# Attention's last batch: the exponents' sums made on TensorE instead of GpSimd

## The reference, cut to what matters

```python
q, k, v = proj(layernorm(x), W_Q, b_Q), proj(ctx, W_K, b_K), proj(ctx, W_V, b_V)
scores = einsum('bhqd,bhkd->bhqk', q, k) / sqrt(32)
attn = softmax(scores, axis=-1)         # over the 512 keys
out = einsum('bhqk,bhkd->bhqd', attn, v)
x = x + tanh(g_xattn[0]) * (out @ W_O + b_O)
# then a quantized FFN, a second attention on the raw context, and a quantized linear layer
```

## Time and profile before

| | us |
|---|---|
| median of 3 runs | 1707.97 (1707.79 to 1710.96) |
| the profiled execution, its own time | 1708.97 |
| its span, first to last instruction | 1707.2 |
| of it up to the end of the attention phase | 839.9 |
| PE busy | 1513.5 (89%) |
| DVE busy | 1233.4 (72%) |
| POOL busy | 905.9 (53%) |
| ACT busy | 873.6 (51%) |

### The profile page before, as it was taken

The page is one execution under the profiler, slowest core; times in us unless marked ns, Lnnn a source line. Parts: engine busy times, 40 slices in busy tenths (PEclk is TensorE's granted clock), DMA queues, the critical chain, the costliest instruction groups (busy, mean ns, idle before and its releaser), DMA issues. The chain is left out here.

```text
span 1707.2 us, 25251 instructions
## 1 busy us (share of the span) xinstructions
PE 1513.5 (89%) x7272; PEld 981.8 (58%) x7305; DVE 1233.4 (72%) x2149; ACT 873.6 (51%) x1433; POOL 905.9 (53%) x1162
## 2 busy tenths in 40 slices
PE   4799999998999999998446899999999939999997
PEld 3556666665656666663135455555555417888885
DVE  3567776777767776666374688888888717999985
ACT  3255555555555555554365545555555415555552
POOL 3168566676658566666301433443444115777774
PEclk9899999999999999997667999999999969999998
DMA  5827456473827456470271444444444353445420
GB/s 187 256 63 207 145 159 194 130 216 111 244 79 204 146 157 198 118 204 13 98 272 37 78 107 113 111 110 106 113 111 110 66 185 118 137 148 182 139 68 37
DMA packets 198430, 233.90 MB, mean 137 GB/s; under 512 B 97196, under 2 KB 114104, under 8 KB 194744
## 3 DMA queue, kind: packets, MB, share of 16 engines
q1 hardware_dynamic: 198328, 232.68, 47.3%
HBM read 135.86 MB, written 75.53 MB: 124 GB/s over the span
## 5 line engine op out<-in xcount | busy, mean ns | idle before, releaser
L510 ACT ACTIVATE a_probs<-a_sc 128x512 f32<-128x512 f32 x512 | 300.3, 596 | 298.7 <-PE a_sc L423 296.2
L565 DVE TENSOR_REDUCE a_negmax<-a_mx 128x1 f32<-128x512 f32 x512 | 338.0, 675 | 99.2 <-PE a_mx L406 98.3
L619 POOL TENSOR_TENSOR a_acc<-a_acc,a_probs 128x512 f32<-128x512 f32 x256 | 320.9, 1283 | 6.0 <-ACT a_probs L510 4.4
L619 POOL TENSOR_TENSOR a_acc<-a_probs 128x512 f32<-128x512 f32 x128 | 161.7, 1284 | 243.5 <-ACT a_probs L510 242.6
L406 PE MATMUL a_mx<-a_stack 96*128 96x512 f32 x512 | 227.0, 443 | 32.9 <-DVE a_negmax L565 20.8
L1002 PE MATMUL bank<-w_wgu,b_xq 128*128 128x512 bf16 x1022 | 227.7, 381 | 7.6 <-DMA b_xq<-b_xcode 7.6
L423 PE MATMUL a_sc<-a_stack 97*128 97x512 f32 x512 | 216.2, 424 | 9.5 <-DMA a_stack<-a_mrow 7.5
L571 DVE RECIPROCAL a_attn<-a_den 128x128 f32<-128x128 f32 x128 | 120.8, 948 | 121.5 <-PE a_den L444 121.5
L1002 PEld LDWEIGHTS bank<-w_wgu,b_xq 128*128 128x128 bf16 x1024 | 100.4, 98 | 130.0 <-DMA b_xq<-b_xcode 8.5
L406 PEld LDWEIGHTS a_mx<-a_stack 96*128 96x128 f32 x512 | 100.8, 197 | 102.1 <-DVE a_negmax L565 51.1
L1041 ACT ACTIVATE b_sig<-bank,b_tok 128x512 f32<-128x512 f32 x128 | 87.6, 684 | 92.4 <-PE bank L1002 89.2
(11 more groups left out here) (177 smaller groups left out, 2733.2 us busy)
## 6 DMA issues: line engine op xcount, KB each, us to landing
a_stack<-spill SPq DMA_DIRECT2D x192, 256.0 KB, 4.9
spill<-a_part SPq DMA_DIRECT2D x64, 512.0 KB, 3.4
ctx_t<-a_ct SPq DMA_DIRECT2D x16, 1024.0 KB, 8.5
c_ct<-ctx_t SPq DMA_DIRECT2D x8, 2048.0 KB, 8.1
a_stage<-in_x_dram SPq DMA_DIRECT2D x32, 256.0 KB, 5.0
a_stage<-in_ctx_dram SPq DMA_DIRECT2D x32, 256.0 KB, 2.7
attn_t<-a_attn SPq DMA_DIRECT2D x32, 256.0 KB, 3.0
b_xin<-in_x_dram SPq DMA_DIRECT2D x32, 256.0 KB, 2.7
```

The lines of the kernel that those rows point to most:

```text
L510: nc.scalar.activation(probs[:, k, j, :], sc[i % 2][:], ACT.Exp, scale=SCALE).then_inc(exp_done, 1)
L565: nc.vector.tensor_reduce(negmax[:, g % 2, j, t:t + 1], mx[i % 2][:], axis=AX.X, op=ALU.max, negate=True).then_inc(mx_done, 1)
L619: nc.gpsimd.tensor_tensor(acc[:, j], probs[:, 0, j] if k == 1 else acc[:, j], probs[:, k, j], ALU.add)\
```

## The change

In the last batch alone, PE makes the whole sum. A new function `add_up(k)` multiplies the block of ones by the exponents of key tile k, four matmuls into the four strips of `den`, accumulating over the key tiles.

```diff
+                def add_up(k):
+                    for j in range(J):
+                        last = nc.tensor.matmul(den[DH * j:DH * (j + 1), :], ones[:], probs[:, k, j, :], start=k == 0, stop=k == T - 1)
+                    return last
...
                     elif name == "pv":
...
+                        if it + shift == NB - 1 and k < T - 1:
+                            if k == 0:
+                                wait_count(pe, recip_done, it, shift, G * T, g * T)
+                                wait_count(pe, mt_done, it, shift, G, min(g + 2, G))
+                            add_up(k)
...
                     elif name == "den":
                         g, = args
+                        if it + shift == NB - 1:
+                            add_up(T - 1).then_inc(den_full, 1)
+                            return
...
                     elif name == "score":       # ACT
-                        wait_count(act, acc_done, it, shift, G * (T - 1) * J, ((g - 1) * (T - 1) + max(k, 1) - 1) * J + j + 1)
+                        if it + shift < NB - 1 or g == 0:
+                            wait_count(act, acc_done, it, shift, G * (T - 1) * J, ((g - 1) * (T - 1) + max(k, 1) - 1) * J + j + 1)
+                        elif k == T - 1 and j == 0:
+                            wait_count(act, den_full, it, shift, G, g)
...
-                    elif name == "acc":         # POOL
+                    elif name == "acc" and it + shift < NB - 1:
```

## The result

The changed kernel takes 1716.05 us (median of 6 runs, 1712.39 to 1720.94), the kernel before, with three more runs beside it, 1708.93 (6 runs, 1707.14 to 1714.24). The ratio of the runs is 1.004, with a 95% interval of 1.0024 to 1.0057: slower by 7 us, between 4 and 10. The prediction was 1716.1, with +8.1 us: the difference is 1 us smaller than forecast, and that the median meets 1716.1 almost to the digit is luck, since the kernel before had 1707.97 when the forecast was made and has 1708.93 with all six runs. The profiled execution has a span of 1714.2 us, 7.0 more than before.

The account below looks back on a forecast made before the run. The last batch was taken as a serial chain of TensorE bursts and scoring stretches. Added sets +10.4, removed GpSimd waits −2.6 and moved waits +0.3 gave +8.1 us, so 1716.1 us, with 8 in 10 for 1712 to 1720.

Parts of the forecast that it names:

- The chain is serial: Last batch: bursts and scoring stretches follow one another, so whatever lengthens a TensorE burst is paid in full.
- The price of a set: Last batch's bursts: four den matmuls of one key tile cost 0.865 us; twelve added sets cost 10.4 us.
- The upper bound of 12.9: Bursts: 0.105 us per change of bank would raise added sets to 12.9 us; dearer sets in general had chance 0.14.
- The removed waits: Before den in groups 1 and 3: waits of 0.75 and 1.83 us for GpSimd's adds go, −2.6 us.
- The moved wait for the copied maxima: Burst starts, groups 0 to 2: first den set waits for the copied maxima, 0.1 us each, +0.3 in all.
- The clock: Last batch: added sets fall on the bursts' upper-clock part, at 0.865 us; time at the lower level does not grow.
- The rise comes inside the burst in every case: Groups 1 to 3: the clock rises within the burst, which begins with 1.1, 4.5 and 3.9 us at the lower level.
- The stretches: Three scoring stretches between bursts: change taken as 0, upper end 1.5 us; lengths near 15.2, 14.5 and 11.0 us.
- The sum: Whole last batch: +8.1 us from added sets, removed waits and moved waits; chance 0.72 for +5.5 to +10.5.
- the clock stays up by denser bursts: Rival, last batch: denser bursts keep the upper clock through the stretches, −1.3 us, 1706.7; chance 0.11, wholly or in part.
- GpSimd was the real bound: Rival, bursts: GpSimd's adds set their length, so removing them pays for the sets; 1706 to 1709 us, chance 0.03.

Follow-up runs that it names:

- e4: Changed kernel with every set of den matmuls in the last batch made twice, sixteen sets more; 1728.58 us, 12.5 over the changed kernel.
- e2: Changed kernel with the last batch's sums left out, only one key tile multiplied by the ones; 1705.59 us, 3.1 under the kernel before.
- e3: Changed kernel with TensorE making the sums in all eight batches, GpSimd adding nothing; 1784.98 us, 76.3 over the kernel before.
- e5: Changed kernel plus one unused full-width matmul behind each score matmul of the last batch's groups 1 to 3; 1709.84 us, 6 under the changed kernel.
- e7: Changed kernel with pv sets of groups 0 to 2 moved behind the next stretch's first four scores, group 3's sets between its scores; 1713.93 us.
- e1: Changed kernel with GpSimd's 48 last-batch adds made as well, their result unused; 1717.16 us, 8.4 over the kernel before.
- e9: Kernel before, GpSimd's sums kept, plus one unused matmul behind each score matmul of the last batch's groups 1 to 3; 1712.63 us.
- e6: Kernel before, but last batch's group 3 summed by TensorE, with den and pv sets of key tiles 0 to 2 between its score matmuls; 1702.45 us.
- e8: Kernel before with group 3's sets between scores; in groups 1 and 2 GpSimd adds three key tiles, with unused matmuls behind scores; 1702.32 us.

## Why the prediction was right, step by step

**The chain is serial.** Right. Sixteen sets more gave +13.1 us of the way (e4), twelve fewer −10.2 (e2), and eighty-four more, those of the seven other batches, +68.9 by the medians (e3), which is 0.82, 0.85 and 0.82 us each.

**The price of a set, 0.865 at the upper clock.** Right: 2.57 us for three (7.00 of e5's burst against 4.43), 10.3 for twelve. The upper bound of 12.9, with a price on each change of bank, is refuted by the even 0.86 between starts above. The Trainium skill ("TensorEngine Tiling (Array Packing)", Key Properties) says that the engine is drained when the tiling mode changes, not when only the tile does. The runs agree on both sides: nothing is paid between `den` and `pv`, and in e7 a set alone between full-width matmuls takes 1.00 us (774.66 to 775.66) instead of 0.86. What the 0.14 us are made of no run separates.

**The removed waits, −2.6.** Right in kind, as e1 (nothing else in GpSimd's work) and e2 bear out, and some 0.3 us too small. The two idle times, 0.75 and 1.83, are counted from modelled ends. In the kernel before, the `pv` matmuls ahead of these waits are

```profile
785.33 4.14 PE L434 MATMUL a_pvb<-a_probs,a_v 128*32 128x512 f32 x32
...
823.41 5.58 PE L434 MATMUL a_pvb<-a_probs,a_v 128*32 128x512 f32 x32
```

and in group 0, where nothing waits, such a row is 3.64 us long and the next starts 3.46 after it, 0.18 before its modelled end. So `den` could have started 3.96 and 5.40 us after these two starts. It started 4.89 and 7.40 after them (790.22 and 830.81), 0.93 and 2.00 late: 2.9 us in all. And the waits are a figure of this clock: e9 has 10.1 us of idle time there.

**The moved wait for the copied maxima.** I took 0.3 us. From the score matmul ahead to the burst's first start it is 0.33 us before and 0.36 after in group 0, and 0.71 and 0.80 in group 2: some 0.1 in all. Group 1 can't be compared, since the clock there differs.

**The clock.** Half right. That longer bursts carry their sets at the upper level held: the time at the lower level in the bursts was 9.5 us before and is 10.1 (0.26 × 2 × 9.43 and 0.27 × 2 × 9.67). "The rise comes inside the burst in every case" was wrong. In group 1 the clock rose ahead of it:

```profile
788.00:789.00 1.00, 1.00 (x5) 0.62 (x4) 0.84 (x2) 0.60 (x1) 0.00 (x0) 0.65 0.00 0
```

That is most of why group 1's burst took 7.01 and not the 7.9 I gave it. Group 3 had more at the lower level (9.67 for 9.3), and group 2 came out as forecast (9.43 for 9.4).

**The stretches.** I left them as they were; they came out 0.71 us shorter together (14.68, 14.61, 10.71 for 15.18, 14.53, 11.00), which I had not forecast. e1 and e4 have them at 15.17, 14.63 and 11.00 with the same sets or more, so the sets are not the cause. The rows show where the time went. In the first stretch TensorE is without a gap from these starts on, the first in the kernel before, the second in the changed one:

```profile
779.78 0.71 PE L406 MATMUL a_mx<-a_stack 96*128 96x512 f32 x1
...
784.40 0.71 PE L412 MATMUL a_mx<-a_stack 96*128 96x512 f32 x1
```

Both stand 9.63 us behind the burst's end. From there to the next burst it takes 5.55 us before and 5.05 after: the clock rose at about 788.7, 0.75 us ahead of the burst, while it rose about 1 us inside the burst before and in e1 and e4. In the last stretch the clock fell 5.7 us behind the burst (0.62 within 826 to 827), and 4.6 to 4.7 before and in e1 and e4, and two scores take 1.18 us at the upper level and 1.48 at the lower one:

```profile
822.87 0.99 PE L429 MATMUL a_sc<-a_stack 97*128 97x512 f32 x2 [0.19 <-ACT a_probs L527]
824.05 0.99 PE L429 MATMUL a_sc<-a_stack 97*128 97x512 f32 x2 [0.20 <-ACT a_probs L527]
...
829.01 1.28 PE L429 MATMUL a_sc<-a_stack 97*128 97x512 f32 x2 [0.20 <-ACT a_probs L527]
830.49 0.79 PE L429 MATMUL a_sc<-a_stack 97*128 97x512 f32 x1 [0.20 <-ACT a_probs L527]
```

Why the clock changed at other moments in this execution no run shows.

**The sum.** Forecast 10.4 − 2.6 + 0.3 = 8.1. Measured in the profile: 10.3 for the sets, 2.9 less for the waits, 0.3 more for time at the lower clock in the bursts, and 0.7 less in the stretches, in which the 0.1 of the moved waits is contained. That makes 7.0, and the way is 6.97 longer. The added sets were right to 0.1 us, the removed waits 0.3 too small and the moved waits 0.2 too large, and the clock, which I took to change nothing, gave 0.5 back. How much the clock gives is a matter of luck in one execution: the three stretches of e1 and e4 are 0.8 us longer together than the changed kernel's.

**The rivals.** That the clock stays up by denser bursts is refuted by e4. Its value was nearly right: I worked out 1706.7 for it, and with the fill the changed kernel takes 1709.8 and a way of 65.9, 0.3 under before, where 1.3 under was forecast. The Trainium skill ("TensorE: Matmul & The Clock Gate", Loop structure matters more than you think) asks for matmuls back-to-back. The traces agree where the stretches are filled (e5, 1.00), and longer bursts alone did not do it (e4, 0.63 to 0.71 in the stretches). That GpSimd was the real bound is refuted for this kernel and true for e9.

## What to carry to other kernels

Before work is moved to the busiest engine because another is "the one waited for", read how long the wait is in front of the consumer: here 2.6 us in a whole phase, against 10.4 us of added matmuls in a place where every other engine waits. Look for a place to put the added work where the chain waits for another engine (e6, e8), and count what lies behind each piece there (e7). An engine hidden by a slow clock turns into the bound when the clock is mended, so price both together (e5, e9). And read pieces of time from start to start: idle time counted from modelled ends was 0.2 us short for each wait.

## What was unexpected of the hardware

One superfluous full-width matmul behind each of 48 scores made the changed kernel 6 us faster (1716.05 to 1709.84), because the granted clock stayed at the upper of its two levels for 66 us (1.00, where the stretches had 0.65 to 0.77). Gaps of no more than 0.2 to 0.7 us between its matmuls preceded the fall to 1.2 GHz, and in the changed kernel TensorE then worked at 1.2 GHz from 806 to 816 us with hardly a gap before the clock rose. And matmuls of 32 columns into two banks in turn keep the same pace as into one, 0.86 us a set of four.
